# A two-layer recurrent kernel: a reordered front with split low products, and a second feed-forward whose first tile moves into the stage before

## What is computed

```
layer 0  xn = layernorm(x)
         delta = shifted(xn) - xn
         low = tanh((xn + delta*mu_x) @ Wx1)         512 -> 5*64
         m_i = low_i @ Wx2_i + bias_i                i = r,w,k,v,g
         r,k,v = (xn + delta*m_i) @ Wr, Wk, Wv       512 -> 256
         w = tanh((xn + delta*m_w) @ Ww_a) @ Ww_b + bw;  g the same with bg
         o_t = r_t (S + bonus k_t v_t);  S = exp(-exp(w_t)) S + k_t v_t
         s = ((groupnorm(o)*ln_w + ln_b) * g * sigmoid(g)) @ Wo
         y = (silu(xn @ Wgate) * (xn @ Wup)) @ Wdown 4-bit, 512 -> 1408 -> 512
         x = x + s * silu(y / rms(y))
layer 1  xn = layernorm(x);  s = linear attention (16 heads, 4 of k and v) @ Wo
         u = relu(xn @ Wup + b + xn @ La @ Lb)       4-bit, 512 -> 2048
         y = u @ Wdown + b' + u @ La' @ Lb'          4-bit, 2048 -> 512
         out = x + s * silu(y)
```

## Time and profile before

| | us |
|---|---|
| three runs | 1621.1, 1625.09, 1626.53; median 1625.09 |
| the profiled execution | 1628.57, its span 1626.8 |
| granted clock, mean | 0.994 |
| end of the front, start of the recurrence's products | 224.02 |
| start of the second feed-forward's products | 1243.28 |

### The profile page before, as it was taken

The page is one execution under the profiler, slowest core; times in us unless marked ns, Lnnn a source line. Parts: engine busy times, 40 slices in busy tenths (PEclk is TensorE's granted clock), DMA queues, the critical chain, the costliest instruction groups (busy, mean ns, idle before and its releaser), DMA issues. The chain is left out here.

```text
span 1626.8 us, 20359 instructions
## 1 busy us (share of the span) xinstructions
PE 1576.9 (97%) x6768; PEld 1136.3 (70%) x6768; DVE 1100.5 (68%) x1584; ACT 438.9 (27%) x735; POOL 626.1 (38%) x482
## 2 busy tenths in 40 slices
PE   7999988999999999999999999999999999999998
PEld 3444456676677676678777777777776678888886
DVE  5787779787887899656457877888877565141422
ACT  2333341222221221322243333333332223131211
POOL 4586649636746568320032332323323331010101
PEclk9999999999999999999999999999999999999999
DMA  5534878757857766240300000000006424020010
GB/s 199 187 116 156 303 263 249 231 194 238 255 180 242 234 213 202 103 169 27 98 26 21 20 20 20 22 18 26 7 29 198 123 91 156 1 92 11 29 50 26
DMA packets 84436, 197.08 MB, mean 121 GB/s; under 512 B 6913, under 2 KB 28673, under 8 KB 76033
## 3 DMA queue, kind: packets, MB, share of 16 engines
q1 hardware_dynamic: 84208, 195.49, 36.4%
q10 hardware_dynamic: 144, 0.52, 0.1%
HBM read 154.05 MB, written 41.94 MB: 120 GB/s over the span
## 5 line engine op out<-in xcount | busy, mean ns | idle before, releaser
L2053 DVE SCALAR_TENSOR_TENSOR l_acc<-l_ps,l_inv,l_acc 128x512 f32<-128x512 f32 x240 | 165.9, 747 | 1.1 <-PE l_ps L773 0.4
L2555 DVE CAST g_x_part<-g_x 128x512 fp32r<-128x512 f32 x64 | 36.5, 570 | 191.7 <-ACT g_x L2606 191.7
L1925 POOL TENSOR_TENSOR relay<-l_expq,l_reluq 128x512 f32<-128x512 f32 x42 | 55.5, 1322 | 183.5 <-ACT l_expq L2198 183.5
L1095 POOL TENSOR_TENSOR r_rS<-r_S,first_r 128x512 f32<-128x512 f32 x64 | 94.3, 1476 | 73.5 <-DVE r_S L1199 73.5
L2488 POOL TENSOR_TENSOR relay<-relay 128x512 f32<-128x512 f32 x16 | 21.8, 1367 | 253.2 <-DVE relay L2536 253.2
L771 PE MATMUL r_ps<-relay_part,entry 128*128 128x512 f32 x256 | 104.0, 406 | 6.0 <-SPq L1034 2.9
L2029 DVE TENSOR_SCALAR l_expq<-l_ps,l_bq 128x512 f32<-128x512 f32 x64 | 48.0, 751 | 86.2 <-ACT l_reluq L2194 86.2
L771 PE MATMUL g_ps<-g_Wdn,g_x_part 128*128 128x512 f32 x256 | 103.1, 403 | 0.0
L1095 POOL TENSOR_TENSOR r_rS<-r_S,r_rT 128x512 f32<-128x512 f32 x64 | 96.9, 1515 | 15.0 <-DVE r_S L1199 15.0
L771 PE MATMUL l_ps<-l_M_part,l_sq_part 128*128 128x512 f32 x256 | 101.6, 397 | 0.8 <-DVE l_acc L2053 0.8
L772 PE MATMUL g_ps<-g_Wdn,g_x_part 128*128 128x512 f32 x256 | 100.6, 393 | 0.0
(11 more groups left out here) (344 smaller groups left out, 4034.1 us busy)
## 6 DMA issues: line engine op xcount, KB each, us to landing
entry<-scratch_wgu SPq DMA_DIRECT2D x32, 1024.0 KB, 9.2
V<-scratch_v SPq DMA_DIRECT2D x96, 256.0 KB
relay<-scratch_x SPq DMA_DIRECT2D x15, 1024.0 KB, 7.7
r_w_part<-scratch_wgu SPq DMA_DIRECT2D x12, 1024.0 KB, 7.9
scratch_wgu<-f_halves SPq DMA_DIRECT2D x24, 384.0 KB, 4.1
relay<-scratch_v SPq DMA_DIRECT2D x32, 256.0 KB
scratch_x<-f_xT SPq DMA_DIRECT2D x4, 1024.0 KB, 6.8
relay<-in_Wq SPq DMA_DIRECT2D x16, 256.0 KB, 2.9
```

Of the source, the lines that this page charges most:

```text
L1095: nc.gpsimd.tensor_tensor(rS[u % RS][:, :], S[u % 2][:, 0:T], rT[u // DK][:, :], ALU.mult).then_inc(rS_ready.sem, 1)
L1925: nc.gpsimd.tensor_tensor(sq[i % N_SQ], expq[i % 2][:, :], reluq[i % 2][:, :], ALU.add).then_inc(sq_ready, 1)
L2053: last = nc.vector.scalar_tensor_tensor(acc[b][:, t, :], ps, scale, acc[b][:, t, :], ALU.mult, ALU.add)
L2555: nc.vector.tensor_copy(hi[:, :], x2[j % 2][:, :]).then_inc(x2_hi_ready.sem, 1)
```

## The change

TensorE's list is reordered: a block now begins with low 1, and the transposes of the next block stand between v and r, `down` behind r. For this xT exists twice (`xTs`), and waits refer to the block before (`shift` in `Ring`). The low products are split: Wx1 is split once at the start by VectorE; x_mu is split in each block by ScalarE (`high_x_mu`) and VectorE (`low_x`), and a low tile is four times `product3`. GpSimd makes `deltas(b+1)` ahead of its remainders, VectorE `mix_x(b+1)` ahead of its second unpacking. In the last block r's first tile comes first, then `down`, then the first half of r's second tile, the decay and gate jobs, and the other half. The front stores g itself; ScalarE makes silu(g) in the recurrence (behind the second gate product; in the last block also behind `square_o`), and VectorE multiplies the two. The loops over b of four engines are written out. Wx1, Wx2 and the bias bg have waits of their own, and bg is loaded behind Wx2.

In the second feed-forward the first up tile is made by TensorE at the end of the linear attention, into the bank next in turn, and the banks are renumbered so that it fits. The up weights are loaded tile by tile, each as soon as its place is consumed, and the down weights likewise.

```diff
-    end_jobs = [("down", 0), ("decay", 0), ("gate", 0), ("decay", 1), ("gate", 1)]
-    jobs = [("xT", kt) for kt in range(KT)] + end_jobs[:1] + [("low", LOWS[0])] + end_jobs[1:]
-    jobs += [("low", m) for m in LOWS[1:]]
+    end_jobs = [("decay", 0), ("gate", 0), ("decay", 1), ("gate", 1)]
+    jobs = [("low", LOWS[0])] + end_jobs + [("low", m) for m in LOWS[1:]]
     jobs += [("mix", *mix) for mix in mix_order[:4 * KT]]
     jobs += [("proj", "k", hh) for hh in range(HH)] + [("mix", *mix) for mix in mix_order[4 * KT:]]
-    jobs += [("proj", s, hh) for s in "vr" for hh in range(HH)]
+    jobs += [("proj", "v", hh) for hh in range(HH)] + [("xT", kt) for kt in range(KT)]
+    jobs += [("proj", "r", hh) for hh in range(HH)] + [("down", 0)]
...
             def sequence(b, last=False):
                 add(b, mix_order[:4 * KT - 1])
                 if not last:
                     deviations(b + 1)
                 add(b, mix_order[4 * KT - 1:])
+                if not last:
+                    deltas(b + 1)
                 n = J_LAST if last else JQ
                 pool.wait_ge(*gu_hi_ready.now(b, 1))
                 for e in range(2):
                     rest = nc.gpsimd.tensor_tensor(halves[e][:, 0:n, 1, :], by_tile(whole[e], n),
                                                    halves[e][:, 0:n, 0, :].bitcast(F32), ALU.subtract)
                 rest.then_inc(gu_lo_ready[0].sem, 1)
-                if not last:
-                    deltas(b + 1)
...
+            def low_x(b, kt):
+                dve.wait_ge(*x_mu_hi_ready.now(b, kt + 1))
+                nc.vector.tensor_tensor(x_mu_lo[:, kt, :], x_mu[:, kt, :], x_mu_hi[:, kt, :].bitcast(F32),
+                                        ALU.subtract).then_inc(x_mu_lo_ready.sem, 1)
+
             def mix_x(b):
 
-                dve.wait_ge(*ring.product_before(("proj", "v", HH - 1), b))
+                dve.wait_ge(*ring.product(("proj", "v", HH - 1), b - 1))
                 for kt in range(KT):
                     dve.wait_ge(*delta_ready.now(b, kt + 1))
                     nc.vector.scalar_tensor_tensor(x_mu[:, kt, :], delta[:, kt, :], mu_x[:, kt:kt + 1],
-                                                   xT[:, kt, 2:T + 2], ALU.mult, ALU.add).then_inc(x_mixed.sem, 1)
+                                                   xTs[b % 2][:, kt, 2:T + 2], ALU.mult, ALU.add).then_inc(x_mixed.sem, 1)
+                    if kt > 0:
+                        low_x(b, kt - 1)
+                low_x(b, KT - 1)
...
                 dve.wait_ge(*ring.product(("proj", "k", HH - 1), b))
                 evacuate(b, mix_order[4 * KT:])
+                mix_x(b + 1)
                 unpack_gate_up(b, 2, 1)
-                mix_x(b + 1)
                 low_gate_up(b)
...
-            dve.wait_ge(small_loaded, 4 * 16)
+            dve.wait_ge(Wx1_loaded, 16)
+            nc.vector.tensor_copy(Wx1_part[0][:, :, :], Wx1[:, :, :]).then_inc(Wx1_hi_ready, 1)
+            dve.wait_ge(Wx1_hi_ready, 1)
+            nc.vector.tensor_tensor(Wx1_part[1][:, :, 0:384], Wx1[:, :, :], Wx1_part[0][:, :, :].bitcast(F32),
+                                    ALU.subtract).then_inc(Wx1_lo_ready, 1)
+            dve.wait_ge(small_loaded, 3 * 16)
             mix_x(0)
...
                     project(b, "v")
-                    low_tanh(b + 1, finally_done, final_place)
+                    act.wait_ge(*stored["x"].now(b - 1, 1))
+                    project(b, "r", [0])
+                    low_tanh(b, finally_done, final_place)
                     decays(b + 1, finally_done, final_place)
                     high_gate_up(b, 1, last_halves, J_LAST)
-                    gate_tanhs(b + 1)
-                    project(b, "r")
+                    project(b, "r", [1])
...
                 high_gate_up(b, 0)
                 normalise(b + 1)
                 project(b, "v")
-                project(b, "r")
                 copy_x(b + 1)
-                low_tanh(b + 1, lambda job: ring.product(job, b + 1), end_place)
+                high_x_mu(b + 1, 0)
+                high_x_mu(b + 1, 1)
+                project(b, "r", [0])
+                high_x_mu(b + 1, 2)
+                high_x_mu(b + 1, 3)
+                project(b, "r", [1])
+                low_tanh(b, lambda job: ring.product(job, b), end_place)
                 high_gate_up(b, 1)
...
+                            product = product3(nc, place[:, :], (Wx1_part[0][:, kt, cols], Wx1_part[1][:, kt, cols]),
+                                               (x_mu_hi[:, kt, :], x_mu_lo[:, kt, :]), kt == 0, kt == KT - 1)
...
+                            if last and job == ("proj", "r", 1) and kt == KT // 2:
+                                for i, end in enumerate(end_jobs):
+                                    pe.wait_ge(*ring.vacated(("xT", i), b))
+                                    end_job(b + 1, end[0], end[1], final_place[end]).then_inc(end_done, 1)
...
+                    if last and job == ("proj", "r", 0):
+                        pe.wait_ge(*ring.vacated(("down", 0), b))
+                        end_job(b, "down", 0, final_place["down", 0]).then_inc(end_done, 1)
...
+            def output_gate(b):
+                act.wait_ge(*g_loaded.before(b, 1))
+                nc.scalar.activation(flat(gate[:, :, :]), flat(gate[:, :, :]), ACT.Silu).then_inc(gate_ready.sem, 1)
...
+            pe.wait_ge(*reader[jobs[len(jobs) - len(banks)]])
+            pe.wait_ge(up_lo_ready, KT)
+            for kt in range(KT):
+                last = product3(nc, banks[len(jobs) % len(banks)][:, :], [q[:, kt, 0:P] for q in kept["up"]],
+                                [q[:, kt, :] for q in x_part[0]], kt == 0, kt == KT - 1)
+            last.then_inc(up_made, 1)
...
+            def load_up(ob, kt):
+
+                sp.wait_ge(expanded, 2 * number["up", ob - 1, kt] + 1)
+                sp.dma_start(up_q[:, kt, :], w["up_q"].rearrange("p (k c) -> p k c", k=KT)[:, kt, ob * C:(ob + 1) * C]).then_inc(
+                    up_loaded[kt], 16)
+
+            def load_down(j):
+                sp.wait_ge(expanded, 2 * number["dn", j - 2] + 1)
+                sp.dma_start(dn_q[:, j % 2, :], w["dn_q"][:, j * C:(j + 1) * C]).then_inc(dn_loaded[j % 2], 16)
...
+            load_up_scale(2)
+            for j in range(UT):
+                if j // 4 + 2 < OB:
+                    load_up(j // 4 + 2, j % 4)
+                    if j % 4 == 3 and j // 4 + 3 < OB:
+                        load_up_scale(j // 4 + 3)
                 if j + 2 < UT:
                     load_down_scale(j + 2)
-                    load_down(j // 2 + 1)
-                    load_down_scale(j + 3)
+                    load_down(j + 2)
...
+                    if n == 0 and first:
+                        pe.wait_ge(up_made, 1)
+                        pe.sem_inc(U.done.sem, 1)
+                    elif n < UT:
```

More of the change, by code:

```diff
@@ L330, in sequence @@
                         sp.dma_start(dst, w[name]).then_inc(hand, 16)
+                    sp.wait_ge(*ring.product(("low", LOWS[-1]), b))
+                    for s in gu_stored:
+                        sp.wait_ge(*s.now(0, 1))
+                    load_entry(0)
                     for s, dst in first_keys.items():
@@ L369, in _ @@
             sequence(0, first=True)
-            with sp.Fori(1, B - 1) as b:
+            for b in range(1, B - 1):
                 sequence(b)
@@ L550, in sequence @@
                 unpack_down(b, 0, J_LAST if last else DQ)
-                if not first:
-                    gates(b)
-                dve.wait_ge(*ring.product(("down", 0), b))
+                dve.wait_ge(*ring.product_before(("down", 0), b))
                 dve.wait_ge(*ring.product(("low", LOWS[-1]), b))
@@ L655, in sequence @@
                 for m in LOWS:
-                    if m == LOWS[1] and not first:
-                        gate_tanhs(b)
                     act.wait_ge(*ring.product(("low", m), b))
@@ L1456, in body @@
                         copy_values(b, j)
+                    if j == 1 and not first:
+                        output_gate(b)
                     if j in parted:
```

228 lines of the change are left out of this document (114 added, 114 removed).

## The result

| | before | changed |
|---|---|---|
| runs, median (us) | 1624.22 of 4 (1621.1 to 1626.53) | 1635.26 of 4 (1631.63 to 1636.83) |
| the profiled execution; its span | 1628.57; 1626.8 | 1631.63; 1629.9 |
| ratio, 95% interval | | 1.0073 [1.005, 1.0095] |

The kernel became slower by 11 us; the forecast of 1627.0 was wrong, and the range ended at 1633.5. Run again in ten more executions (e10) it stood at 1.0049 [1.0029, 1.0070], 8 us; the two intervals overlap between 1.005 and 1.007. Ratios here compare fast executions alone: one execution of the kernel before, timed beside e9 to e12, took 2250.05 us at a granted clock of 0.654 and is in none of them.

The account below looks back on a forecast made before the run. TensorE was taken to bound the front block at 50.45 us, the VectorE/GpSimd ring 3.1 us behind. Front +8.4 and second feed-forward -6.5 sum to +1.9 us: 1627.0 from 1625.09, range 1616.5 to 1633.5.

Parts of the forecast that it names:

- The front, +8.4: Whole front: predicted 8.4 us slower, from periods +3.1, start +1.2 and end +4.1.
- periods: Front: three distances between blocks' first evacuations on VectorE, predicted 52.2 us each, together +3.1 over 153.55.
- tail: End of the front: r's first half and a bank wait delay down and the decays, +4.1 us, bounds 0 and +5.8.
- The ring: Front: chain from xn through ScalarE copies, GpSimd deltas and remainders, store, high part and VectorE's work; period 52.2 us.
- E: Front: the moment of a block's first evacuation on VectorE, from which times in the block are counted.
- I take four of the six: Front: four of six ops in the ring, deltas and remainders, each lengthened 0.44 us, giving a period of 52.2.
- rival 3: Front: split low products meet TensorE's lower clock after the new wait and save nothing; 0 to 2 us, within the forecast.
- The second feed-forward, -6.5: Second feed-forward: 6.5 us faster, from -3.0, +0.8 and -4.3; bounds -4 and -8.4.
- The pieces: Second feed-forward: loading weights in quarters removes VectorE's wait for the 1 MB load and a short one, -4.3 us.
- -3.0 for barrier and clock, +0.8 for VectorE's start: Second feed-forward: early up tile shortens the barrier wait and keeps the clock, -3.0 us; VectorE's later expansions cost 0.8.
- Rival 2: Front: store ring bounds it, all six GpSimd ops lengthened, if remainders end after E+38.3; +7.8 us, 1633; chance 0.26.
- Rival 1: Front: GpSimd ops not lengthened, v copied early, periods 50.1 to 50.5; total -7.0 or better, 1618; chance 0.32.

Follow-up runs that it names:

- e10: The changed kernel itself, run again beside the kernel before: 1633.93 us, ratio 1.0049.
- e9: Kernel before, with only the second feed-forward's weights loaded tile by tile: 1620.9 us, ratio 0.9983.
- e12: Kernel before, with only the split low products and the loads that had to move for them: 1631.29 us, ratio 1.0039.
- e2: Changed kernel, with the linear attention and second feed-forward of the kernel before, so front only: 1635.36 us, ratio 1.0066.
- e3: Changed kernel, with down, decay and gate jobs ahead of both r tiles in the front's last block: 1629.91 us, ratio 1.0036.
- e5: Changed kernel, with r's first tile between v and the transposes in TensorE's list: 1634.01 us, ratio 1.0057.
- e1: Kernel before, with the linear attention's end and second feed-forward of the changed kernel: 1623.54 us, ratio 0.9986.
- e8: Kernel before, with the first up tile made in the linear attention, weight loads as before: 1622.9 us, ratio 0.9981.
- e13: e1, with the four stores of the attention's sums issued later, in the second feed-forward: 1619.0 us, ratio 0.9967.
- e6: Changed kernel, with the altered orders of e3, e4 and e5 together: 1622.23 us, ratio 0.9984.
- e4: Changed kernel, with GpSimd's remainders ahead of deltas again: 1634.27 us, ratio 1.0051.
- e7: Changed kernel, with low tiles as one f32 product each again, no split: 1637.81 us, ratio 1.0075.
- e11: e6, with the four stores of the attention's sums issued behind loads of the second feed-forward's tiles 1 and 2: 1619.73 us, ratio 0.997.

## Why the prediction was wrong

**The front, +8.4: right in the first profiled execution, too small in most.** Start +0.7 (predicted +1.2), periods +3.0 (+3.1), tail +4.9 (+4.1), together +8.6. The ring was followed as it is: `xn` at E+26.7, deltas 4.9 and remainders 4.5 us (lengthened beside each other's VectorE work), 6.1 from store to high part, period 51.8 to 52.6. "I take four of the six" is borne out by the sum (9.4 us for the six in block 1 against 7.8 alone, 1.6 longer where I took 1.8), not op by op. Three further traces of this front as it stands, or with the tail alone altered (e2, e3, e10), have sums of 157.6, 158.3 and 158.9, up to 2.3 more. The step that failed here is in rival 3, where a lower clock after the new wait hits the low tiles and "in the middle blocks the other ring hides that". The clock reaches the transposes and r, not the low tiles alone, up to 2.9 us in a block. The other ring hid half of it in e2's block 1 (period 52.98 for 51.76) and less in e10's (54.00). The tail's term, +4.1, was 0.8 too small in every trace of that order (+4.9, and +5.4 in e5). By the times of e2 the front costs 10.7 us, 2.3 more than predicted.

**The second feed-forward, -6.5: it was -2.5**, and this is the step that failed by most. From the attention's first product with `l_M_part` to the end it took 793.31 us before and 790.79 after (789.05 to 794.38 in the seven other traces that have it), and e1's times give -2.3. The pieces were sized well: -4.3 predicted, -4.15 behind tile 4 in e9's trace. The term "-3.0 for barrier and clock, +0.8 for VectorE's start" failed: at the barrier TensorE did gain what was said (1.05 us of wait, clock at 1.00), and gave back all of it at tile 4, for the reason that I had priced at 0.8. I had not followed VectorE's chain from the barrier to tile 4: from its first expansion at 1250.64 three steps of 5.68 us, a wait of 2.2 us for a down weight, and 3.4 us for the fourth weight through ScalarE and GpSimd, which begins at the barrier whatever TensorE has done ahead of it. The wait of 2.20 us then cost another 1.5 by the clock, which is one of three outcomes seen.

**Why +3.1 between the profiled executions looked like +1.9.** No term of the sum used the recurrence, and the forecast added its difference to the median, so the 3.5 us by which the profiled execution of before lay over its median did no harm to it. They flattered it afterwards. A part of them is in TensorE's waits in the recurrence:

```profile
PE r_ps L771 <- DMA entry<-scratch_wgu: 2.4, 4, 1.1
PE r_ps L771 <- DMA r_w_part<-scratch_wgu: 2.1, 1, 2.1
```

From the recurrence's first product to the attention's it took 475.72 us, where e1, e8, e9 and e13 with the same front took 474.25, 469.60, 471.22 and 472.02, and the changed kernel 471.70. These 4 us are chance, not the change; a difference taken from one execution that has them hides as much of a loss. The miss is then made up so: against +1.9, the ten executions of e10 stood at +8.4, 6.5 more, of which the second feed-forward has about 4 and the front about 2. The first four executions stood at +11.0 (1635.26 less 1624.22); the last 2.6 lie within the scatter between the two sets, whose intervals overlap.

**The rivals.** Rival 2, slower, named the sign and nearly the time (1633), but not the place: the remainders ended at E+37.5, ahead of its point of E+38.3. Rival 1, a front that keeps its saving, needed the orders of e6, where periods were 49.9 to 51.0 and the tail 41.2. That its tail would be mended by copying v early I didn't try; moving the end jobs did it.

**The shared port.** Here the trace came nearer to the page than I had it. A subtraction of VectorE took 0.68 us alone (e4), 1.52 beside a delta and 2.31 beside a remainder, 1.6 longer, which is almost the whole 1.79 of a remainder alone. By "SBUF — State Buffer" of the Trainium skill (Summary: rules for kernel authors) the second one fully blocks. For VectorE's side that describes the 2.31; GpSimd's four deltas in 4.93 us grew by 0.2 each and not by 0.7, so in these rows it is mostly VectorE that waits. The sum of 1.78 that I took from the rule is its worst case, in which an op waits for the whole of the other; a delta of 1.48 doesn't speak against it.

## What to carry to other kernels

Before taking work off the busiest engine, ask whose result it waits for: here the split saved 2.5 us of TensorE a block and put four subtractions on the chain that TensorE waits for, and the fastest kernel has the new order without the split. When two rings lie within 3 us of each other, undoing one step at a time can show nothing; change both before judging either. A gain ahead of a barrier is real only if the next thing that TensorE needs isn't made by an engine that starts at the barrier, and a wait of 2 us should be charged with what the clock may do behind it (here 0 to 4.4 us).

## What the runs showed of the hardware

- A wait of TensorE of 1.6 to 2.6 us, then short ones of 0.2 to 0.4, was followed by the lower of its two clocks (1.2 and 2.4 GHz; f32 transposes in 2.1 to 3.04 us for 1.64) in 17 of the 18 such blocks of six traces (changed, e2, e3, e4, e7, e10). The same wait of 2.11 us at 107.33 in the changed kernel's trace, the one exception, and at 107.32 in e2's ended differently. The 2.7 us at the change of stages brought 0.83 before, and 1.00 in e9.
- A small load suffered from large stores issued just before: a 256 KB load issued at 1253.95, behind 4 MB of stores, with the DMA engines moving 392 GB/s, landed 11.7 us later; the median of such loads from issue to landing was 3.3 us. With the stores issued later (e11) the wait for it was gone.
- Executions of the kernel before scatter by 10 us at nearly the same mean clock, from 1621.0 (0.995) to 1631.6 (0.992) in one set of 23; for differences under 0.5% one profiled execution of each is not enough.
